# Two-half cross attention in wide steps, three low parts in four on GpSimd and the fourth on VectorE

## The chip, the cores and the metric

The kernel runs on one core of a Trainium2 chip. The metric is the device time of one execution in microseconds (us); a lower figure is better. TensorE (PE) multiplies, VectorE (DVE), ScalarE (ACT) and GpSimd (POOL) work on elements, and SyncE (SP) issues the DMAs.

## The reference

Three residual blocks follow each other on x of 8 batches x 64 queries x 2048 features. The change is in the first one:

```
x = x + xattn(layernorm(x), ctx)      # ctx: 8 x 1601 keys x 2048
    a = einsum('bqd,bkd->bqk', query, key)
    e = softmax(a)
    c = einsum('bqk,bkd->bqd', e, key)   # the keys are the values too
x = x + self_attention(layernorm(x))  # causal, 32 heads, 64 tokens a batch
x = x + lora_experts(layernorm(x))    # rank-8 experts with top-16 gates
```

Everything is float32. Each float32 operand of a large product is split in two: a high part rounded to the format that TensorE multiplies fast (fp32r), and a low part, operand minus high part. The products of the parts are summed in PSUM.

## The kernel before

**Tiling.** The 1601 keys of a batch are three blocks of 512 (4 tiles of 128 keys) and a tail of 65 keys. For the scores the features must lie on the partitions, so each 128 x 128 tile of the context is transposed by TensorE into PSUM (`ps_t`, a ring of 4 banks); ScalarE copies the bank to `ct_hi`, VectorE subtracts that from the bank into `ct_lo`, and two matmuls (`score`, L656 and L657) multiply both with the transposed queries. A slot is one such set: 4 transposes, one copy, one subtraction of 128 x 512, two matmuls of 512 columns. There are 48 slots a batch and 3 for the tail, and 5 more for the queries and the exponentials. `LAG` is 3: the score of a slot stands three slots behind its transposes.

**Natural pieces.** For the second product the keys are used as they lie in memory, in 52 units a batch of one tile x 512 features: ScalarE writes `nat_hi` (L416), GpSimd writes `nat_lo` (L372), and `product` (L680, L681) has two matmuls of 512 columns a unit. For every thirteenth unit, and every second one near the end, VectorE makes both parts (L561, L562). The ring has 8 units.

**Softmax.** It runs online over the three blocks: a maximum per block, a running maximum (L511), exponentials, and `alpha` to rescale. The upper 64 partitions of every product hold the part from the low weights; each block and column group (512 features) is added to `acc` in SBUF (L527, L532). At the end of a batch the upper half is copied down (L436), added (L576), divided by the row sum and added to x (L577).

**Order.** The order on each engine is written out by hand from the table `TRANS` and runs as a loop over batches 1 to 6 with batch 0, batch 7 and an end turn written out around it. The two other blocks of the kernel follow behind a barrier: `self_attention` starts by loading the last 128 rows of x1 and with the layer norm of all rows. Row statistics of the first 384 rows (L590) are computed in the end turn of the cross attention.

Of the kernel before, what the change touches and what calls it, by code (L numbers as in the profile page):

```python
# [34 lines left out]
SHARE, SHARED = 13, (5,)

END_SHARED = 32


def transposes():  # L40

    base = [("c", 0, c) for c in range(DC)] + [("t", k) for k in range(len(TAILS))]
# [4 lines left out]
    base.insert(31, ("e", 0))  # L50
# [2 lines left out]


TRANS = transposes()
NT = len(TRANS)
assert NT % RING == 0
Q1_AT, E2_AT = TRANS.index(("q", 1)), TRANS.index(("e", 2))
SCORE_STEPS = NBLK * DC + len(TAILS)

SPANS = [(0, 0, BLK, 0, DC), (0, BLK, BLK + TAIL, 1, DC + len(TAILS)),
         (1, 0, BLK, 0, 2 * DC + len(TAILS)), (2, 0, BLK, 1, SCORE_STEPS)]


UNITS = [(j, c, k) for j in range(NBLK) for c in range(NCOL) for k in range(KT + (j == 0))]
NU = len(UNITS)
# [5 lines left out]
EIGHTS = NAT * (NU % (NAT - 1))
assert (NU - EIGHTS) % (NAT - 1) == 0


def nat_slot(u):
    return u % NAT if u < EIGHTS else (u - EIGHTS) % (NAT - 1)


def nat_reuse(u):

    return NAT if NAT - 1 <= u < EIGHTS + NAT - 1 else NAT - 1


def unit_slots():

    at = [[] for _ in range(NT)]

    def spread(units, prev, lo, hi):
        for n, u in enumerate(units):
            at[int(lo + n * (hi - lo) / len(units))].append((u, prev))

    spread(range(FIRST_OF[1] + C1_NOW, FIRST_OF[2]), True, 0, 12)
    spread(range(FIRST_OF[2], NU), True, 12, 34)
    spread(range(0, FIRST_OF[1]), False, 34, 54)
    spread(range(FIRST_OF[1], FIRST_OF[1] + C1_NOW), False, 54, NT)
    return at


UNITS_AT = unit_slots()
NATURAL_AT = [[] for _ in range(NT)]
for _s in list(range(LEAD, NT)) + list(range(LEAD)):

    NATURAL_AT[(_s - LEAD) % NT] += [(_u, _prev and _s >= LEAD) for _u, _prev in UNITS_AT[_s]]
LAST_SLOT = {UNITS[u][:2]: s for s, us in enumerate(UNITS_AT) for u, _ in us if LAST_OF[UNITS[u][:2]] == u}

HALF_AT, READ_AT = {22: 0, 25: 1, 42: 2, 3: 3}, {23: 0, 26: 1, 43: 2, 4: 3}
STATS_AT, EXP_AT, SUM_AT = {26: 0, 43: 1, 4: 2}, {28: 0, 45: 1, 6: 2}, 9  # L110

FOLD_AT = {LAST_SLOT[NBLK - 1, c] + 2: c for c in range(NCOL)}
# [1454 lines left out]
```

## Time and profile before

| | |
|---|---|
| median of 3 runs | 1874.06 us (1871.58 to 1874.44) |
| profiled execution, its span | 1873.4 us |
| cross attention, from its first wide copy to its last score | 14.2 to 665.1 us |
| its end, to the first instruction of self attention | 665.1 to 711.8 us |
| self attention and feed forward | 711.8 to 1873.4 us |
| mean granted clock of TensorE | 0.97 |

The span of the profiled execution lies within the three times. Shares of busy time are an average over the three blocks, which have different limits; the stretches above are to be read by themselves. In a timeline the durations of neighbouring matmuls overlap, so what one costs is the distance from its start to the next start.

### The profile page before, as it was taken

The page shows a single profiled execution, that of the slowest core. Times are in us where ns is not written, and L with a number is a line of the kernel's source. Part 1 is how long each engine was busy: PE and PEld are TensorE (multiplying, and loading weights), DVE is VectorE, ACT ScalarE, POOL GpSimd, SP SyncE. Part 2 cuts the span into 40 slices and gives each one's busy share as a digit, 9 for nine tenths or more (in the row PEclk, how much of TensorE's full clock was granted, in tenths as well). Part 3 has the DMA queues.
Part 4 walks back from the last instruction along what each step waited for, and adds up shares of the span by engine and source line. Part 5 has one row for each costly group of instructions (what it writes and reads, how often), then busy time and mean ns, then how long its engine had stood idle before and what let it go on. Part 6 is the DMA issues. An engine that isn't in the chain of part 4 may idle for free. (4 is left out here: it accounts for less than half of the span.)

```text
span 1873.4 us, 25168 instructions
## 1 busy us (share of the span) xinstructions
PE 1731.9 (92%) x8781; PEld 1400.3 (75%) x8781; DVE 901.3 (48%) x1408; ACT 762.8 (41%) x1237; POOL 887.0 (47%) x474
## 2 busy tenths in 40 slices
PE   7898999989899963999999999999999999978999
PEld 6687877878687742788788887888878788756677
DVE  6898999989998997010220301203012030135523
ACT  4687877778777732122122221221222212110321
POOL 0778777787877762234434344333333333312010
PEclk9999999999999975999999999999999999979999
DMA  9356465555546314132232322323222332311113
GB/s 315 101 192 203 143 215 157 179 168 190 184 151 203 102 67 123 47 88 90 91 89 90 90 90 90 90 90 90 86 93 71 106 92 67 102 55 48 45 68 113
DMA packets 174921, 218.87 MB, mean 117 GB/s; under 512 B 3848, under 2 KB 102152, under 8 KB 171784
## 3 DMA queue, kind: packets, MB, share of 16 engines
q1 hardware_dynamic: 174880, 218.32, 36.3%
q8 instruction: 26, 0.43, 0.1%
q14 instruction: 15, 0.12, 0.0%
HBM read 209.92 MB, written 8.39 MB: 117 GB/s over the span
## 5 line engine op out<-in xcount | busy, mean ns | idle before, releaser
L905 POOL TENSOR_TENSOR sa_w_lo<-sa_raw,sa_w_hi 128x2048 fp32r<-128x2048 f32 x80 | 367.9, 4599 | 624.7 <-ACT sa_w_hi L919 624.7
L372 POOL TENSOR_TENSOR xa_nat_lo<-xa_raw,xa_nat_hi 128x512 fp32r<-128x512 f32 x231 | 309.8, 1362 | 96.6 <-ACT xa_nat_hi L416 95.3
L1045 DVE TENSOR_TENSOR rows<-rows,sa_ps_mm 128x512 f32<-128x512 f32 x128 | 88.1, 688 | 494.0 <-PE sa_ps_mm L759 494.0
L757 PE MATMUL sa_ps_mm<-h_hi,sa_w_hi 128*128 128x512 f32 x768 | 303.9, 396 | 1.4 <-DVE h_lo L980 1.4
L758 PE MATMUL sa_ps_mm<-h_lo,sa_w_hi 128*128 128x512 f32 x768 | 300.0, 391 | 0.0
L759 PE MATMUL sa_ps_mm<-h_hi,sa_w_lo 128*128 128x512 f32 x768 | 300.0, 391 | 0.0
L493 DVE TENSOR_TENSOR xa_ct_lo<-xa_ps_t,xa_ct_hi 128x512 fp32r<-128x512 f32 (+2 forms) x408 | 269.8, 673 | 54.4 <-ACT xa_ct_hi L395 43.7
L395 ACT ACTIVATE xa_ct_hi<-xa_ps_t 128x512 fp32r<-128x512 f32 (+2 forms) x408 | 238.5, 588 | 108.1 <-PE xa_ps_t L628 101.2
L919 ACT ACTIVATE sa_w_hi<-sa_raw 128x2048 fp32r<-128x2048 f32 x80 | 153.0, 1913 | 287.1 <-PE sa_ps_mm L759 287.1
L656 PE MATMUL xa_ps_s<-xa_ct_hi,xa_q_t 128*128 128x512 f32 x384 | 185.5, 483 | 40.6 <-DVE xa_ct_lo L493 35.6
L757 PE MATMUL sa_ps_mm<-sa_w_hi,sa_o_hi 128*128 128x512 f32 x512 | 204.3, 399 | 6.9 <-ACT sa_q_t L951 4.8
L758 PE MATMUL sa_ps_mm<-sa_w_lo,sa_o_hi 128*128 128x512 f32 x512 | 203.3, 397 | 0.0
L759 PE MATMUL sa_ps_mm<-sa_w_hi,sa_o_lo 128*128 128x512 f32 x512 | 203.2, 397 | 0.0
L372 POOL TENSOR_TENSOR xa_nat_lo<-rows,xa_nat_hi 128x512 fp32r<-128x512 f32 x112 | 157.0, 1420 | 87.7 <-ACT xa_nat_hi L416 87.6
L680 PE MATMUL xa_ps_o<-xa_nat_hi,xa_e_t 128*128 128x512 f32 (+1 forms) x416 | 173.8, 418 | 14.6 <-DVE xa_nat_lo L562 7.4
L757 PEld LDWEIGHTS sa_ps_mm<-h_hi,sa_w_hi 128*128 128x128 f32 x768 | 144.9, 189 | 35.4 <-ACT sa_v_t L951 2.3
L759 PEld LDWEIGHTS sa_ps_mm<-h_hi,sa_w_lo 128*128 128x128 f32 x768 | 144.8, 189 | 30.7
L758 PEld LDWEIGHTS sa_ps_mm<-h_lo,sa_w_hi 128*128 128x128 f32 x768 | 145.0, 189 | 29.1
L681 PE MATMUL xa_ps_o<-xa_nat_lo,xa_e_t 128*128 128x512 f32 (+1 forms) x416 | 166.5, 400 | 0.0
L628 PE MATMUL xa_ps_t<-xa_ident,xa_raw 128*128 128x128 f32 x1024 | 154.3, 273 | 0.0
L628 PEld LDWEIGHTS xa_ps_t<-xa_ident,xa_raw 128*128 128x128 f32 x1024 | 126.7, 140 | 33.9 <-issue 0.2
L657 PE MATMUL xa_ps_s<-xa_ct_lo,xa_q_t 128*128 128x512 f32 x384 | 151.8, 395 | 0.0
(184 smaller groups left out, 2450.0 us busy)
## 6 DMA issues: line engine op xcount, KB each, us to landing
xa_raw<-in_ctx SPq DMA_DIRECT2D x64, 1024.0 KB, 5.0
rows<-in_ctx SPq DMA_DIRECT2D x32, 1024.0 KB, 5.6
sa_raw<-in_L_attn_w_q SPq DMA_DIRECT2D x32, 1024.0 KB, 5.8
sa_raw<-in_L_attn_w_o SPq DMA_DIRECT2D x32, 1024.0 KB, 4.9
sa_raw<-in_L_attn_w_k SPq DMA_DIRECT2D x8, 1024.0 KB, 5.1
sa_raw<-in_L_attn_w_v SPq DMA_DIRECT2D x8, 1024.0 KB, 5.0
xa_raw_tail<-in_ctx SPq DMA_DIRECT2D x8, 520.0 KB
xa_xq<-in_x SPq DMA_DIRECT2D x8, 512.0 KB, 4.8
```

Source lines behind the costliest of these rows:

```text
L372: pool.tensor_tensor(nat_lo[0:rows, nat_slot(u), :], src, nat_hi[0:rows, nat_slot(u), :].bitcast(F32), ALU.subtract).then_inc(nat_pool, 1)
L395: act.activation(ct_hi[:, bank, 0:w], ps_t[:, bank, 0:w], ACT.Copy).then_inc(hi_done, 1)
L493: dve.tensor_tensor(ct_lo[:, bank, 0:w], ps_t[:, bank, 0:w], ct_hi[:, bank, 0:w].bitcast(F32), ALU.subtract).then_inc(lo_done, 1)
L628: ins.append(pe.transpose(ps_t[:, bank, k * P:(k + 1) * P], piece(j, g // KT)[:, k, g % KT * P:(g % KT + 1) * P], ident[:]))
L656: pe.matmul(o, q_t[:, g, :], ct_hi[:, bank, :], start=g == 0, stop=False)
L680: pe.matmul(o, e_t[0:rows, j, k, :], nat_hi[0:rows, nat_slot(u), :], start=k == 0, stop=False)
L681: pe.matmul(o, e_t[0:rows, j, k, :], nat_lo[0:rows, nat_slot(u), :], start=False, stop=u == LAST_OF[j, c]).then_inc(pv_done, 1)
L757: pe.matmul(out, hi, mov_hi, start=first, stop=False)
L758: pe.matmul(out, hi, mov_lo, start=False, stop=False)
L759: return pe.matmul(out, lo, mov_hi, start=False, stop=last)
L905: pool.tensor_tensor(w_lo[:, n, :], raw[:, n, :], w_hi[:, n, :].bitcast(F32), ALU.subtract).then_inc(w_lo_done, 1)
L919: act.activation(w_hi[:, n % 2, :], raw[:, n % 2, :], ACT.Copy).then_inc(w_hi_done, 1)
```

## The change

The cross attention is written anew; the other two blocks are the same, except for line numbers. `rsqrt_steps` of the cross attention has 3 iterations for 4.

- The keys of a batch are two halves: 833 keys (4 tiles of 128, 3 of 107) and 768 (6 of 128). A step transposes one feature tile of a whole half: 7 or 6 transposes into a slot of two banks, one copy and one subtraction of 833 or 768 columns, and 4 score matmuls (512 and 322, or 512 and 256 columns, for the high and the low part). There are 32 steps a batch for 51 slots. The ring `ps_t` has 2 slots for 4, and `LAG` is 2.
- Transposes of queries and exponentials ride in the spare columns of a step's slot (`SIDE`), with no slot of their own.
- Natural pieces are made as pairs of tiles, 128 x 1024 (or 107 x 1024), 26 a batch, in a ring of 4 pairs. ScalarE makes every high part. The low part is GpSimd's, but VectorE's for each pair with number u % 4 == 2 and for the last 8.
- The softmax has two parts a batch for three. The first half's product goes to `acc` by ScalarE. VectorE rescales it into the PSUM bank of the second half's product (`rescale`), ScalarE copies the upper half out (`low`), and VectorE adds it (`fold`) and divides and adds x (`finish`), all with one operand in PSUM. The running maximum is a `tensor_scalar`.
- The result is stored by column group. The code is written out for all 8 batches, with no loop.
- The 12 row statistics of x1 stand behind everything else of the cross attention on VectorE.

The core of the diff:

```diff
-NBLK = 3
-KT = 4
-RING = 4
-LAG = 3
-SHARE, SHARED = 13, (5,)
-NAT = 8
+HALVES = 2
+TILES = [[128] * 4 + [107] * 3, [128] * 6]
+RING = 2
+LAG = 2
+NAT = 4
+ENDING = before_half(STAGES - 1, PAIRS_OF) + NAT
+ON_DVE = [u >= ENDING or u % 4 == 2 for u in range(len(PAIR_ORDER))]
...
-        ps_t = ps("xa_ps_t", [P, RING, 512])
-        ps_s = ps("xa_ps_s", [P, 2, 512])
+        ps_t = ps("xa_ps_t", [P, RING, 1024])
+        ps_s = ps("xa_ps_s", [P, 1024])
         ps_o = ps("xa_ps_o", [P, 2, 512])
...
+            for u, (h, n) in enumerate(PAIR_ORDER):
+                if ON_DVE[u]:
+                    continue
+                src, p = pair(h, n)
+                pool.wait_ge(nat_act, u + 1)
+                pool.tensor_tensor(nat_lo[0:p, u % NAT, :, :], src, nat_hi[0:p, u % NAT, :, :].bitcast(F32),
+                                   ALU.subtract).then_inc(nat_pool, 1)
...
+            def rescale(b, c):
+                dve.wait_ge(pv_done, uses_before(HALVES * b + 1) + GROUP_END[1][c] + 1)
+                dve.wait_ge(first_out, NCOL * b + c + 1)
+                dve.scalar_tensor_tensor(out=group_bank(c), in0=acc[:, column(c)], scalar=alpha[:, 0:1], in1=group_bank(c),
+                                         op0=ALU.mult, op1=ALU.add).then_inc(rescaled, 1)
+            def fold(b, c):
+                dve.wait_ge(low_ready, NCOL * b + c + 1)
+                dve.tensor_tensor(ps_o[0:LQ, c % 2, :], ps_o[0:LQ, c % 2, :], low[:, c % 2, :], ALU.add).then_inc(folded, 1)
+            def natural_low(u, h, n):
+                src, p = pair(h, n)
+                dve.wait_ge(nat_act, u + 1)
+                dve.tensor_tensor(nat_lo[0:p, u % NAT, :, :], src, nat_hi[0:p, u % NAT, :, :].bitcast(F32),
+                                  ALU.subtract).then_inc(nat_dve, 1)
...
+                if t == ALL_STEPS - 1:
+                    dve.wait_ge(rows_in, 16 * (RT - 1))
+                    for r in range(RT - 1):
+                        for c in range(NCOL):
+                            dve.bn_stats(row_bn[:, r, c, :], x1_rows[:, r, column(c)])
...
+            for t in range(ALL_STEPS):
+                if t == LAG:
+                    first_queries()
+                if t % DC == 2:
+                    for h, i in USE_AT.get(t, []):
+                        product(h, i)
+                if LAG <= t < STEPS + LAG:
+                    score_step(t - LAG)
+                if t < STEPS:
+                    i = transpose_step(t)
+                if t in SIDE:
+                    i = side_step(t)
+                if t < STEPS or t in SIDE:
+                    i.then_inc(t_done, 1)
+                if t % DC != 2:
+                    for h, i in USE_AT.get(t, []):
+                        product(h, i)
```

On TensorE, in the middle of a batch, the rows before are slots of four transposes, two scores (L656, L657) and one unit (L680, L681), here at the end of batch 0's turn:

```order
L628 MATMUL xa_ps_t<-xa_ident,rows 128x128 x4
L648 REGISTER_ALU
L656 MATMUL xa_ps_s<-xa_ct_hi,xa_q_t 128x512
L657 MATMUL xa_ps_s<-xa_ct_lo,xa_q_t 128x512
L673 REGISTER_ALU
L678 REGISTER_ALU
L680 MATMUL xa_ps_o<-xa_nat_hi,xa_e_t 128x512
L681 MATMUL xa_ps_o<-xa_nat_lo,xa_e_t 128x512
```

The rows now, in the second half of a batch: a step's four scores (L611), the six transposes of a later step (L574), four more transposes of queries that ride along (L583), and a pair of units (L631).

```order
L611 MATMUL xa_ps_s<-xa_ct_hi,xa_q_t 128x512
L611 MATMUL xa_ps_s<-xa_ct_hi,xa_q_t 128x256
L611 MATMUL xa_ps_s<-xa_ct_lo,xa_q_t 128x512
L611 MATMUL xa_ps_s<-xa_ct_lo,xa_q_t 128x256
L574 MATMUL xa_ps_t<-xa_ident,xa_raw_b 128x128 x6
L583 MATMUL xa_ps_t<-xa_ident,xa_xq 128x64 x4
L631 MATMUL xa_ps_o<-xa_nat_hi,xa_e_t 128x512
L631 MATMUL xa_ps_o<-xa_nat_lo,xa_e_t 128x512
L631 MATMUL xa_ps_o<-xa_nat_hi,xa_e_t 128x512
L631 MATMUL xa_ps_o<-xa_nat_lo,xa_e_t 128x512
```

The same columns go through in fewer and larger groups; only one group of transposes stands between a step's transposes and its score, for two before.

On VectorE, within a batch before (L493 is the subtraction for the scores, L561 and L562 the two parts of a unit, L576 and L577 the finish of a column group):

```order
L532 SCALAR_TENSOR_TENSOR xa_acc<-xa_acc,xa_alpha,xa_ps_o 128x512
L493 TENSOR_TENSOR xa_ct_lo<-xa_ps_t,xa_ct_hi 128x512
L561 CAST xa_nat_hi<-rows 128x512
L562 TENSOR_TENSOR xa_nat_lo<-rows,xa_nat_hi 128x512
L493 TENSOR_TENSOR xa_ct_lo<-xa_ps_t,xa_ct_hi 128x512
L576 TENSOR_TENSOR xa_res<-xa_acc,xa_res 64x512
L577 SCALAR_TENSOR_TENSOR xa_res<-xa_res,xa_total,xa_xr 64x512
L493 TENSOR_TENSOR xa_ct_lo<-xa_ps_t,xa_ct_hi 128x512 x4
```

And now (L524 is that subtraction, L494 `rescale`, L499 `fold`, L505 `finish`, L511 the low part of a pair, L455 the normalization of the next queries):

```order
L511 TENSOR_TENSOR xa_nat_lo<-xa_raw_a,xa_nat_hi 107x1024
L455 TENSOR_SCALAR xa_xq<-xa_xq,xa_mv,xa_rs_w 64x512
L524 TENSOR_TENSOR xa_ct_lo<-xa_ps_t,xa_ct_hi 128x768
L527 TENSOR_TENSOR xa_e_t<-xa_ps_t,xa_e_t 107x3x64
L494 SCALAR_TENSOR_TENSOR xa_ps_o<-xa_acc,xa_alpha,xa_ps_o 128x512
L455 TENSOR_SCALAR xa_xq<-xa_xq,xa_mv,xa_rs_w 64x512
L524 TENSOR_TENSOR xa_ct_lo<-xa_ps_t,xa_ct_hi 128x768
L499 TENSOR_TENSOR xa_ps_o<-xa_ps_o,xa_low 64x512
L524 TENSOR_TENSOR xa_ct_lo<-xa_ps_t,xa_ct_hi 128x768
L505 SCALAR_TENSOR_TENSOR xa_acc<-xa_ps_o,xa_total,xa_xr 64x512
L524 TENSOR_TENSOR xa_ct_lo<-xa_ps_t,xa_ct_hi 128x768
```

The finish has its operand in PSUM in place of two in SBUF, and the one operation with both operands in SBUF that is left, besides the normalization with its one, is L511.

On VectorE at the end of the cross attention before, the row statistics (L590) stand between the last units and finishes; L712 is the first instruction of self attention:

```order
L590 BN_STATS row_bn<-rows 128x6 x2
L532 SCALAR_TENSOR_TENSOR xa_acc<-xa_acc,xa_alpha,xa_ps_o 128x512
L576 TENSOR_TENSOR xa_res<-xa_acc,xa_res 64x512
L577 SCALAR_TENSOR_TENSOR xa_res<-xa_res,xa_total,xa_xr 64x512
L590 BN_STATS row_bn<-rows 128x6 x2
L532 SCALAR_TENSOR_TENSOR xa_acc<-xa_acc,xa_alpha,xa_ps_o 128x512
L576 TENSOR_TENSOR xa_res<-xa_acc,xa_res 64x512
L577 SCALAR_TENSOR_TENSOR xa_res<-xa_res,xa_total,xa_xr 64x512
```

And now, with L558 for the statistics and L659 for the first instruction of self attention:

```order
L505 SCALAR_TENSOR_TENSOR xa_acc<-xa_ps_o,xa_total,xa_xr 64x512
L494 SCALAR_TENSOR_TENSOR xa_ps_o<-xa_acc,xa_alpha,xa_ps_o 128x512
L499 TENSOR_TENSOR xa_ps_o<-xa_ps_o,xa_low 64x512
L505 SCALAR_TENSOR_TENSOR xa_acc<-xa_ps_o,xa_total,xa_xr 64x512
L558 BN_STATS row_bn<-rows 128x6 x12
L204 UNCONDITIONAL_BRANCH
L914 UNCONDITIONAL_BRANCH
L659 BN_AGGR sa_mv<-row_bn 128x2 x3
```

All twelve now stand behind the last finish.

## Rows read from the trace of the kernel before

**Rows 1.** The page: busy time of each engine over the span

```profile
PE 1731.9 (92%) x8781; PEld 1400.3 (75%) x8781; DVE 901.3 (48%) x1408; ACT 762.8 (41%) x1237; POOL 887.0 (47%) x474
```

**Rows 2.** Windows: length, then busy us by engine; the first is one batch long

```profile
185.90:268.55 82.65, 77.59 (x471) 62.94 (x470) 76.13 (x123) 63.30 (x123) 65.03 (x49) 1.00 0.55 176
...
14.20:665.10 650.90, 610.27 (x3686) 496.36 (x3686) 586.16 (x920) 492.11 (x955) 488.15 (x363) 1.00 0.54 176
665.10:711.80 46.70, 21.24 (x60) 12.00 (x59) 40.65 (x57) 10.68 (x20) 18.71 (x13) 0.69 0.14 48
```

**Rows 3.** Waits from 103.6 to 678.1 us: total, times, longest

```profile
PEld xa_ps_s L656 <- DVE xa_ct_lo L493: 40.4, 33, 1.8
...
PEld xa_ps_t L639 <- issue: 7.9, 21, 0.7
```

**Rows 4.** Timeline of TensorE: one slot with a unit, then tail pieces

```profile
301.48 0.60 PE L628 MATMUL xa_ps_t<-xa_ident,xa_raw 128*128 128x128 f32 x4
301.84 0.48 PE L656 MATMUL xa_ps_s<-xa_ct_hi,xa_q_t 128*128 128x512 f32 x1
302.15 0.39 PE L657 MATMUL xa_ps_s<-xa_ct_lo,xa_q_t 128*128 128x512 f32 x1
302.38 0.40 PE L680 MATMUL xa_ps_o<-xa_nat_hi,xa_e_t 128*128 128x512 f32 x1
302.62 0.39 PE L681 MATMUL xa_ps_o<-xa_nat_lo,xa_e_t 128*128 128x512 f32 x1
302.85 0.60 PE L628 MATMUL xa_ps_t<-xa_ident,xa_raw 128*128 128x128 f32 x4
...
31.57 0.54 PE L634 MATMUL xa_ps_t<-xa_ident,xa_raw_tail 66*128 66x66 f32 x6
31.91 0.48 PE L656 MATMUL xa_ps_s<-xa_ct_hi,xa_q_t 128*128 128x512 f32 x1
...
34.47 0.28 PE L662 MATMUL xa_ps_s<-xa_ct_hi,xa_q_t 128*128 128x66 f32 x1
34.58 0.28 PE L663 MATMUL xa_ps_s<-xa_ct_lo,xa_q_t 128*128 128x66 f32 x1
```

**Rows 5.** Groups by form: count, busy us, mean ns

```profile
L493 DVE TENSOR_TENSOR xa_ct_lo<-xa_ps_t,xa_ct_hi 128x512 fp32r<-128x512 f32 x384 | 258.6, 684 | 53.9 <-ACT xa_ct_hi L395 43.2
L395 ACT ACTIVATE xa_ct_hi<-xa_ps_t 128x512 fp32r<-128x512 f32 x384 | 227.4, 595 | 105.9 <-PE xa_ps_t L628 101.2
L489 DVE TENSOR_TENSOR xa_e_t<-xa_ps_t,xa_e_t 128x256 fp32r<-128x256 f32 x24 | 10.0, 417 | 1.6
L395 ACT ACTIVATE xa_ct_hi<-xa_ps_t 128x330 fp32r<-128x330 f32 x16 | 7.0, 440 | 1.5 <-PE xa_ps_t L634 0.7
```

**Rows 6.** Single lines: duration in ns, least, median and most

```profile
L577 DVE SCALAR_TENSOR_TENSOR xa_res<-xa_res,xa_total,xa_xr x32: 744/1658/1671, 117.2 to 706.4; 64x512 f32<-64x512 f32 x32
L511 DVE TENSOR_TENSOR xa_run_max<-xa_run_max,xa_mx x16: 151/1791/2434, 68.1 to 672.3; 64x1 f32<-64x1 f32 x16
L532 DVE SCALAR_TENSOR_TENSOR xa_acc<-xa_acc,xa_alpha,xa_ps_o x64: 721/737/746, 91.3 to 704.3; 128x512 f32<-128x512 f32 x64
L372 POOL TENSOR_TENSOR xa_nat_lo<-xa_raw,xa_nat_hi x231: 1264/1293/1768, 75.9 to 694.3; 128x512 fp32r<-128x512 f32 x116
L905 POOL TENSOR_TENSOR sa_w_lo<-sa_raw,sa_w_hi x80: 4503/4602/4624, 724.2 to 1701.4; 128x2048 fp32r<-128x2048 f32 x80
```

**Rows 7.** Windows of L561, then of L562, over seven batches

```profile
103.60:678.10 574.50, 30.96 (x32) 0.99 0.52 170
...
103.60:678.10 574.50, 31.23 (x32) 0.99 0.52 170
```

**Rows 8.** Timeline of VectorE at the end, and the next block's start

```profile
689.59 1.28 DVE L590 BATCH_NORM_STATS2 row_bn<-rows 128x6 f32<-128x512 f32 x2
...
706.45 0.74 DVE L577 SCALAR_TENSOR_TENSOR xa_res<-xa_res,xa_total,xa_xr 64x512 f32<-64x512 f32 x1
711.85 0.51 DVE L712 BATCH_NORM_AGGREGATE sa_mv<-row_bn 128x2 f32<-128x24 f32 x3 [4.66 <-PEq L160]
```

More of the change, by code:

```diff
@@ L55 @@
[L55 to L68, printed above, removed]
@@ L69 @@
-C1_NOW = 2
-NAT = 8
[L74 to L98, printed above, removed]
-    return at
@@ L102 @@
[L102 to L112, printed above, removed]
@@ new lines, with pair_units, products @@
+NAT = 4
+def pair_units():
+    first = []
+    for c in range(0, NCOL, 2):
+        first += [(c, 0), (c, 2), (c, 4), (c, 6), (c + 1, 0), (c + 1, 2), (c + 1, 4)]
+    second = [(c, k) for c in range(NCOL) for k in (0, 2, 4)]
+    return [first, second]
+def products():
+    out = []
+    for x in range(HALVES):
+        units = {v: n for n, v in enumerate(PAIRS[x])}
+        uses = []
+        for c in range(NCOL):
+            both = [(c, units[c, k], [(k, 0), (k + 1, 1)]) for k in (0, 2, 4)]
+            if x == 0:
+                odd = [(c, units[c - c % 2, 6], [(6, c % 2)])]
+                both = both + odd if c % 2 == 0 else odd + both
+            uses += both
+        out.append(uses)
+    return out
@@ new lines, with before_half @@
+PAIRS = pair_units()
+USES = products()
+PAIRS_OF, USES_OF = [len(p) for p in PAIRS], [len(u) for u in USES]
+LAST_USE = [[max(i for i, v in enumerate(USES[x]) if v[1] == n) for n in range(PAIRS_OF[x])] for x in range(HALVES)]
+GROUP_END = [[max(i for i, v in enumerate(USES[x]) if v[0] == c) for c in range(NCOL)] for x in range(HALVES)]
+def before_half(h, per_half):
+    return sum(per_half) * (h // HALVES) + per_half[0] * (h % HALVES)
+PV_AT = 6
+E_PARTS = [[(4, 0, 4), (5, 4, 7)], [(4, 0, 2), (5, 2, 4), (6, 4, 6)]]
@@ new lines, with evacuations, side_count, product_steps @@
+SIDE = side_transposes()
+def evacuations(t):
+    return min(t, STEPS) + 1
+def side_count(what, n, k):
+    return next(evacuations(t) for t, v in SIDE.items() if v[0] == what and v[1] == n and v[2] <= k < v[3])
+def product_steps():
+    at, step_of = {}, {}
+    for h in range(STAGES):
+        n = USES_OF[h % HALVES]
+        for i in range(n):
+            t = DC * (h + 1) + PV_AT + (i * DC // n if h < STAGES - 1 else i)
+            at.setdefault(t, []).append((h, i))
+            step_of[h, i] = t
+    return at, step_of
@@ L292, in links_per_turn, with column, uses_before, pair @@
-        def links_per_turn():
-            own = sum(shared(0, u) for u in range(NU))
-            return own + (1 + 2 + 2) + 3 + NCOL + (1 + 1 + RSQRT_LINKS)
+        def column(c):
+            return slice(c * 512, (c + 1) * 512)
+        def uses_before(h):
+            return before_half(h, USES_OF)
+        def pair(h, n):
+            x = h % HALVES
+            c, k = PAIRS[x][n]
+            if k == 6:
+                return raw[x][0:TILES[x][k], c:c + 2, k, :], TILES[x][k]
+            return raw[x][0:TILES[x][k], c, k:k + 2, :], TILES[x][k]
@@ L354, in _ @@
-            turns(sp, turn)
-            sp.wait_ge(stored, 16 * B)
+                for h, c in groups_before(t, 4):
+                    b, x = divmod(h, HALVES)
+                    if x == 1:
+                        sp.wait_ge(finished, NCOL * b + c + 1)
+                        sp.dma_start(x1[b * LQ:(b + 1) * LQ, column(c)], acc[0:LQ, column(c)]).then_inc(stored[c], 16)
+                        if c == NCOL - 1 and b + 1 < B:
+                            load_rows(b + 1, xr, xr_in)
+            for c in range(NCOL):
+                sp.wait_ge(stored[c], 16 * B)
@@ L594, in _ @@
[L594 to L604 removed]
+            for i in layernorm_links():
+                link(i)
+            for c in range(NCOL):
+                normalize(c)
```

745 lines of the change are left out of this document (323 added, 422 removed).

## The prediction

> **What bounds the kernel now.** I read the page first [rows 1]: TensorE is busy 92% of the span, but that is a mean over three blocks, and the change is in one of them. So I cut the span into windows [rows 2]. The cross attention takes 650.9 us for its copies and scores and 46.6 us for its end; the 1161.6 us behind it are two blocks whose code the change leaves alone. One batch takes 82.65 us here; I use 82.4, a little under it, as 650.9 us over eight are 81.4 and the first batch starts without products, and there VectorE is busy 76 us (92%), TensorE 77.6, GpSimd 65 and ScalarE 63. TensorE's busy time counts overlaps, so I count its work by starts in the timeline [rows 4]: four transposes and what follows to L656 take 0.36 us, L656 0.31, L657 and each matmul of a unit 0.23. A slot without a unit is 0.90 us. Six tail transposes take 0.34 us, and a 66-column matmul 0.11.
>
> A batch on TensorE is then 48 x 0.90 = 43.4 us for slots, 16 x 0.057 = 0.9 us for tail transposes, 32 x 0.11 = 3.5 us for tail scores, 104 x 0.23 = 23.9 us for units, and 29 small transposes, priced like the wide ones at 0.09 us, 2.6 us: 74.3 us. Against 82.4 us that leaves 8.1 us in which TensorE waits or is held up. The waits [rows 3] say for whom: L656 waits 40.4 us over seven batches (5.8 us each) for the subtraction `xa_ct_lo` on VectorE, and 7.9 us (1.1 each) are issue gaps at the exponentials. So two things set the pace: TensorE's own columns, and hold-ups on VectorE that outlast the ring.
>
> What holds VectorE up is in the single lines [rows 6]. L577 can take 744 ns and has a median of 1658; L511 works on one column, can take 151 ns and has a median of 1791. Both have all operands in SBUF. L532, with one operand in PSUM, is 721 to 746 ns in all 64 cases. The extra time looks like a wait for the end of a GpSimd instruction, which takes 1293 ns.
>
> **The change, part by part.**
>
> *TensorE.* A 833-column step has 7 transposes, scores of 512, 322, 512 and 322 columns; 322 columns at 0.23 us for 512 are 0.145 us, 256 are 0.115. Transposes cost between 0.0875 us (0.35/4) and the 0.11 us of the narrow matmul [rows 4]. The step is 7 x 0.0875 + 0.31 + 0.145 + 0.23 + 0.145 = 1.44 us at the low end and 1.52 at the high end; the 768-column step 1.295 to 1.35. Sixteen of each are 43.8 to 45.9 us, for 47.8 before. Units and small transposes stay at 26.5. A batch is 70.3 to 72.4 us; I take 71.3, a saving of 3.0 us.
>
> *VectorE, without hold-ups.* By the slope between 256 and 512 columns [rows 5], 1.04 ns a column, the subtractions are 1.02 and 0.95 us; back to back about 0.08 us of each vanishes (two L590 of 0.68 take 1.28 us [rows 8]). 32 of them are 29 us for 33: 4 less. From the 76 us go further 8.9 us for L561 and L562 (62.2 over seven batches [rows 7]), 3.6 for the hold-ups of four L577 (1658 - 744 ns), 3.3 for those of two L511, and 5.2 for eight of the twelve 128 x 512 operations on `acc` (0.65 each; L532 shows the size), of which ScalarE takes four and the third block four: 76 - 4 - 8.9 - 3.6 - 3.3 - 5.2 = 51 us, in which the remaining hold-ups of the normalization still are. One block less in the softmax is offset by wider instructions. The new low parts are 6.5 a batch of 1024 columns, 0.68 + 512 x 1.04 ns - 0.08 = 1.14 us: 7.4. The sum is 58 to 59 us.
>
> *VectorE's hold-ups.* Left are 6.5 low parts and 4 normalizations a batch that have all operands in SBUF. A GpSimd instruction of 1024 columns, between the 1293 ns for 512 and the 4602 for 2048 [rows 6], is 1.29 + 512 x 2.15 ns = 2.4 us. The bounds of a hold-up are nothing, if GpSimd has just finished, and 2.4 us. A pair comes every 2.8 to 3 us (26 a batch), longer than 2.4, so GpSimd often is through when VectorE's turn (u % 4 == 2) comes. I take 0.6 us each, 6 us a batch; VectorE then has 65 us, under TensorE's.
>
> *ScalarE.* By the slope between 330 and 512 columns [rows 5], 0.85 ns, a step's copy is 0.87 or 0.81 us, and a pair's high part 1.05. With about 0.1 us less when back to back: 24 + 25 us, softmax and side pieces 6, new copies of `acc` and `low` 4, 59 us for 63. It stays under the rest, but a step on it with a pair and a copy to `low` (0.8 + 1.0 + 0.5 = 2.3 us) is as long as a step.
>
> *The ring.* This is what the change gives away. Between a step's transposes and its score TensorE now has the products of a step (0.75), a score (0.8), transposes (0.7) and products (0.75): 3.0 us. The two evacuations need 0.1 + 0.87 + 1.02 = 2.0, so 1.0 us is spare. Before it was three slots of 1.37, 4.1 us, against 1.4: 2.7 spare. Hold-ups of a microsecond, hidden before, now reach TensorE. I charge per batch: 1.0 us for each of two softmax steps, in which ScalarE waits for VectorE's maximum with the next copy behind it; 0.5 us for each of the 6.5 steps with a low part on VectorE; 1 us for pairs late from GpSimd; 1.1 us of issue gaps as before. That is 7.4 us, for 8.1 now. Its bounds are 1 us (the issue gaps alone) and more than today's, below.
>
> A batch is 71.3 + 7.4 = 78.7 us, against 82.4: 3.7 x 8 = 30 us saved.
>
> *The end.* Before, 42.1 us pass from the last score (665.1) to the end of the last finish (707.2), and 4.6 us from there to self attention (711.85) [rows 2, 8]. Now: softmax 4.5 us (copy 0.8, add 0.9, maximum 1.4, exponentials 1.0, hops), exponentials transposed and split 2 us, then 12 uses. Four pairs are ready; the other eight need ScalarE (1.05) and VectorE, whose eight low parts and twelve other operations are 9 + 8 us, with waits for the banks in between some 22 us. The last finish ends about 29 us behind the last score, 13 us earlier. Behind it come the 12 statistics, 12 x 0.6 = 7.2 us, which lay in gaps before; the store runs beside them, and the barrier (taken as half of the 4.6 us) follows. That gives back 5 us. Net: 8 us saved, with bounds 0 and 12.
>
> *Nothing.* The first wide copy waits for the first layer norm as before; the context's data are the same bytes, and 176 GB/s over the stretch [rows 2] leave the DMA under six tenths busy. The pieces come back 7 steps (16 us) before they are needed. If that cover were gone, a late piece would cost its transfer, 1.6 MB at 176 GB/s or 9 us.
>
> **Sum.** 30 + 8 = 38 us off the profiled 1873.4, and the profiled execution is 0.7 us under the median: 1836 us. A time within 0.2% (3.7 us) of before can't be told from no change.
>
> **Rivals.**
>
> *A. VectorE becomes the bound (slower).* The low parts and normalizations meet GpSimd in mid-instruction each time. 10.5 hold-ups of up to 2.4 us are 25 us; with 59 of work and 2 us of waits for ScalarE a batch takes 86 us, 3.6 more than now: +29, less 8 at the end, 1895 us. It decides from a mean hold-up of about (82.4 - 59 - 2) / 10.5 = 2.0 us. For it speaks that L511's median is longer than a whole GpSimd instruction [rows 6]; against it, that GpSimd has 19.5 pairs x 2.4 = 47 us of work in 79, where before it was 65 in 82 [rows 2]. The Trainium skill (SBUF — State Buffer, "SBUF: two separate sides") says that VectorE and GpSimd share a port pair as an exclusive lock for a whole instruction, the loser blocked; the trace agrees with it in L511 and L577, and taken at its worst, with each meeting a full one, it is this rival. The same page excepts what runs on VectorE's own ports; L532 at 721 to 746 ns agrees.
>
> *B. The shallow ring eats the saving.* Waits rise from 8.1 to about 10.5 us a batch, since every hold-up over 1 us shows. A batch is 81.8 us: 5 + 8 saved, 1861 us. For it: the spare falls from 2.7 to 1.0 us. Against: half of the hold-ups go away.
>
> *C. The waits nearly vanish.* With VectorE at 65 and ScalarE at 59 us nothing but TensorE's columns is left, 71.3 + 3.5: 61 + 8 saved, 1804 us. For it: the waits before were for VectorE alone [rows 3]. Against: steps of ScalarE and VectorE as long as TensorE's own.
>
> **How the numbers follow.** My forecast (78.7 us a batch, its own range 1815 to 1852) has 0.50, B 0.20, C 0.13, A 0.17. The predicted time is the forecast's. For 8 in 10 the range takes B whole and the upper half of C, and of A the mild third: 1802 to 1885. Of B a quarter falls within 0.2%: same 0.05. Slower is A, 0.17, with 0.01 for B's edge: 0.18. Faster 0.77.
>
> **What would show it.** Right: a batch of 77 to 80 us in the windows; L532's kind at 0.74 us, fold and finish without hold-ups; 1024-column GpSimd instructions of 2.4 us; twelve statistics in some 7 us behind the last finish. Wrong: the low parts on VectorE with a median over 2.5 us (A), waits for `xa_ct_lo` above 8 us a batch (B), or waits under 3 us (C). Pairs waited for from GpSimd by more than 2 us a batch would say that a lead of four pairs is too little, which I charged at 1 us only.

## The result, and the profile after

The changed kernel takes 2526.08 us (median of 4 runs, 2525.89 to 2527.45), the kernel before 1874.21 (4 runs, 1871.58 to 1874.44): 1.349 times as long, 95% interval 1.347 to 1.351. The forecast was 1836, the range 1802 to 1885, and no rival ended above 1895. The transfers, which the prediction put down at nothing, set the time of the first block.

The page of the changed kernel, the same rows as in [rows 1] and those that changed most (parts 1, 2, 5 and 6):

```profile
PE 1797.7 (71%) x8781; PEld 1477.0 (59%) x8781; DVE 778.9 (31%) x1130; ACT 752.6 (30%) x928; POOL 736.5 (29%) x250
...
PEclk8587686876967769678696899999999999998999
DMA  2321232322423224232233222232322232231012
GB/s 78 96 77 56 96 109 64 122 75 73 132 64 118 79 73 130 63 104 81 66 133 101 67 84 85 83 98 83 100 83 86 87 93 83 83 100 67 36 67 100
...
L574 PE MATMUL xa_ps_t<-xa_ident,xa_raw_a 128*128 128x128 f32 (+1 forms) x896 | 144.9, 314 | 560.5 <-DMA xa_raw_a<-in_ctx 560.5
...
xa_raw_a<-in_ctx SPq DMA_DIRECT2D x32, 642.0 KB
...
xa_xq<-in_x SPq DMA_DIRECT2D x8, 512.0 KB, 38.7
```

Over the first 1320 us, which are the cross attention but for its end, TensorE is busy 51% and each of the other engines under 40%. TensorE stood 560.5 us in front of the transposes of the first half, waiting for a DMA. Yet the DMA engines are busy two or three tenths. Many loads cannot be the cause; a load that few of them carry can. The 642 KB load is the one of the three tiles of 107 keys.

Two windows, the first one batch long, as in [rows 2] (busy us of PE, PEld, DVE, ACT and POOL, granted clock, DMA share, GB/s); the second view, apart, is the DMA from 200 to 260 us in 40 slices:

```profile
570.73:730.61 159.88, 85.71 (x471) 71.67 (x471) 61.44 (x88) 61.62 (x84) 47.44 (x21) 0.77 0.29 92
...
350.00:360.00 10.00, 7.72 (x48) 6.40 (x46) 4.87 (x6) 6.41 (x9) 7.23 (x4) 1.00 0.07 26
```

```profile
GB/s 25 26 26 26 134 385 194 25 26 26 26 25 26 26 26 25 26 26 26 25 26 26 26 55 310 339 33 26 26 25 37 26 26 25 26 26 26 25 26 26
```

A batch takes 159.9 us, where it took 82.65. Between short peaks above 300 GB/s the transfer rate is flat at 26 GB/s, with 0.07 of sixteen engines busy. One in sixteen is 0.06, so one engine is carrying everything. 642 KB at 26 GB/s are 25 us, four times a batch, 32 in all. On trn2 the Trainium skill ("DMA: Bandwidth & Descriptors", "Why a DMA increments its semaphore by 16 and not by 1") gives a rule of which I took no account: a hardware-issued copy goes over the largest number of engines, 16 at most, that divides the outermost dimension of both its patterns. By that rule a load over 107 partitions, a prime number, has one engine; the trace agrees.

The waits of the changed kernel from 100 to 1200 us, as in [rows 3] (total, times, longest), and the queue of SyncE (start, length of the issue):

```profile
PE xa_ps_t L574 <- DMA xa_raw_a<-in_ctx: 440.4, 25, 19.8
DVE xa_bn L445 <- DMA xa_xq<-in_x: 174.8, 7, 71.0
...
PEld xa_ps_s L611 <- DVE xa_ct_lo L524: 60.5, 14, 49.9
```

```profile
183.26 54.13 SPq L323 DMA_DIRECT2D xa_raw_a<-in_ctx  x6
237.44 25.08 SPq L326 DMA_DIRECT2D xa_xq<-in_x  x1
```

The second damage is in the queue. Six issues took 54 us and the one of the query rows behind them 25 more, although these rows are small and land 5.1 us after their issue in the median where no such load is ahead of them (the kernel with 112 rows below). Here they land 38.7 us after it, VectorE waits for them (174.8 us), and behind that wait in VectorE's order stand the low parts that TensorE needs. The granted clock is 0.77 in this batch, and TensorE's busy time 85.7 us for the 77.6 before. Two rows of its timeline show why, the first behind a wait of 16.9 us, the second four microseconds on. The granted clock is 0.50 (1.2 GHz) from 215 to 219 us and 0.98 (2.4 GHz) from 219.5 to 221.5; from their start to the next matmul the same seven transposes take 1.31 us at the lower level and 0.65 at the higher:

```profile
215.26 1.62 PE L574 MATMUL xa_ps_t<-xa_ident,xa_raw_a 128*128 128x128 f32 x7 [16.85 <-DMA xa_raw_a<-in_ctx]
...
219.66 0.88 PE L574 MATMUL xa_ps_t<-xa_ident,xa_raw_a 128*128 128x128 f32 x7
```

At the end the statistics and the barrier are to be seen. VectorE's timeline, as in [rows 8] (start, length, count, idle before and releaser):

```profile
1356.40 0.74 DVE L505 SCALAR_TENSOR_TENSOR xa_acc<-xa_ps_o,xa_total,xa_xr 64x512 f32<-64x512 f32 x1
1357.07 7.20 DVE L558 BATCH_NORM_STATS2 row_bn<-rows 128x6 f32<-128x512 f32 x12
1364.58 0.69 DVE L659 BATCH_NORM_AGGREGATE sa_mv<-row_bn 128x2 f32<-128x24 f32 x3 [0.30 <-PEq L204]
```

### The profile page after: what moved, and what is told of

Read it like the earlier page. It is cut to its first block and busy times, and to the rows that moved or that the text cites. A ratio compares the mean times of both kernels' runs of the same rounds, so it can differ in the third digit from the quotient of the medians.

```text
span 2524.2 us, 21640 instructions
## 1 busy us (share of the span) xinstructions
PE 1797.7 (71%) x8781; PEld 1477.0 (59%) x8781; DVE 778.9 (31%) x1130; ACT 752.6 (30%) x928; POOL 736.5 (29%) x250
## 5 line engine op out<-in xcount | busy, mean ns | idle before, releaser
L574 PE MATMUL xa_ps_t<-xa_ident,xa_raw_a 128*128 128x128 f32 (+1 forms) x896 | 144.9, 314 | 560.5 <-DMA xa_raw_a<-in_ctx 560.5
L574 PEld LDWEIGHTS xa_ps_t<-xa_ident,xa_raw_a 128*128 128x128 f32 (+1 forms) x896 | 130.8, 172 | 577.2 <-issue 569.9
L413 ACT ACTIVATE xa_ct_hi<-xa_ps_t 128x833 fp32r<-128x833 f32 (+1 forms) x256 | 214.7, 839 | 781.0 <-PE xa_ps_t L574 590.3
L524 DVE TENSOR_TENSOR xa_ct_lo<-xa_ps_t,xa_ct_hi 128x833 fp32r<-128x833 f32 (+1 forms) x256 | 252.9, 988 | 613.9 <-ACT xa_ct_hi L413 407.1
L374 POOL TENSOR_TENSOR xa_nat_lo<-xa_raw_a,xa_nat_hi 128x1024 fp32r<-128x1024 f32 (+1 forms) x84 | 199.9, 2388 | 440.7 <-ACT xa_nat_hi L388 440.7
L374 POOL TENSOR_TENSOR xa_nat_lo<-xa_raw_b,xa_nat_hi 128x1024 fp32r<-128x1024 f32 x66 | 158.3, 2403 | 535.6 <-ACT xa_nat_hi L388 535.4
L611 PE MATMUL xa_ps_s<-xa_ct_hi,xa_q_t 128*128 128x512 f32 (+2 forms) x512 | 156.7, 390 | 81.8 <-DVE xa_ct_lo L524 59.5
L631 PE MATMUL xa_ps_o<-xa_nat_hi,xa_e_t 128*128 128x512 f32 (+1 forms) x416 | 201.8, 485 | 8.9 <-DVE xa_acc L505 6.3
L631 PE MATMUL xa_ps_o<-xa_nat_lo,xa_e_t 128*128 128x512 f32 (+1 forms) x416 | 181.0, 435 | 0.0
L611 PEld LDWEIGHTS xa_ps_s<-xa_ct_hi,xa_q_t 128*128 128x128 f32 x512 | 99.9, 209 | 116.7 <-DVE xa_ct_lo L524 62.3
## 6 DMA issues: line engine op xcount, KB each, us to landing
xa_xq<-in_x SPq DMA_DIRECT2D x8, 512.0 KB, 38.7
```

Source lines behind the costliest of these rows:

```text
L374: pool.tensor_tensor(nat_lo[0:p, u % NAT, :, :], src, nat_hi[0:p, u % NAT, :, :].bitcast(F32), ALU.subtract).then_inc(nat_pool, 1)
L413: i = act.activation(ct_hi[:, t % RING, 0:w], ps_t[:, t % RING, 0:w], ACT.Copy)
L524: i = dve.tensor_tensor(ct_lo[:, t % RING, 0:w], ps_t[:, t % RING, 0:w], ct_hi[:, t % RING, 0:w].bitcast(F32), ALU.subtract)
L574: i = pe.transpose(ps_t[:, t % RING, OFFS[x][k]:OFFS[x][k] + p], raw[x][0:p, c, k, g % 4 * P:(g % 4 + 1) * P], ident[0:p, 0:p])
L611: i = pe.matmul(ps_s[:, lo:hi], q_t[:, g, :], ct[:, t % RING, lo:hi], start=g == 0 and ct is ct_hi, stop=g == DC - 1 and ct is ct_lo)
L631: ins = pe.matmul(group_bank(c), e_t[0:p, x, k, :], nat[0:p, u % NAT, half, :], start=first and (k, half) == tiles[0] and nat is nat_hi, s ...
```

## Experiments

**One engine, two, fifteen, sixteen.** Theory: the number of rows decides the number of engines. Rivals: three tiles in one load, the shape of the pieces, or sheer DMA traffic. In the first kernel each 107-row load is two, of 96 and 11 rows, and TensorE waits for the count of both (as in the two other splits, its line is left out here):

```diff
-    sp.dma_start(raw[x][0:p, c, k0:k1, :], keys_of(b, x, c, k0, k1, p)).then_inc(raw_in[x][c], 16)
+    for lo, hi in (((0, 96), (96, 107)) if p == 107 else ((0, p),)):
+        sp.dma_start(raw[x][lo:hi, c, k0:k1, :], keys_of(b, x, c, k0, k1, p)[lo:hi]).then_inc(raw_in[x][c], 16)
```

> The load of the 107-row tiles in two DMAs, 96 and 11 rows; nothing else. Theory (a DMA over 107 partitions runs on one DMA engine, 26 GB/s, and 32 of them in a row set the time): the waits of the transposes for the DMA go, and the time falls from 2526 to what the blind working gave, 1802 to 1885 us. Rival 1 (the wide steps with a ring of two are slow by themselves and the loads are only asked for late): still above 2300 us. Rival 2 (two DMAs a piece choke SyncE's queue): three are worse, above 2526 us.

Measured: 1873.68 us (10 runs), ratio to before 1.0005 (0.9995 to 1.0015). The whole loss of 652 us is gone, and besides the load and that count nothing was touched.

In the second the load stays one, with 112 rows; the five extra rows are read and not used:

```diff
+    if p == 107:
+        first = src.ap[0]
+        src = bass.AP(src.tensor, src.offset, [[first[0], 112]] + [list(d) for d in src.ap[1:]])
+        p = 112
```

> The same tiles in one DMA over 112 partitions, 5 rows more than are used. Theory: 112 = 7 x 16 spreads over all engines, so like the split in 96 and 11 within 10 us, with one DMA fewer a piece. Rival 1: above 2300 us. Rival 2 (number of DMAs): exactly as slow as the changed kernel, 2526 us, since the number is the same.

Measured: 1870.02 us (10 runs), ratio 0.9981 (0.9972 to 0.9991). More bytes, 656 us less. I call this one the cured kernel.

The third splits in 106 rows and 1:

> The same tiles in DMAs of 106 rows and 1 row. If the number of engines is the largest one up to 16 that divides the number of partitions, 106 = 2 x 53 gives two engines: some 12 us for each of these loads, 49 us a batch, with 25 us more on those engines for their part of the rest: 74 us a batch, about the length of a batch, and a time between 1840 and 2000 us. If any split of the 107 rows cures it, the time is that of 96 and 11. If only a multiple of 16 is fast and all others run on one engine, about 2520 us.

Measured: 2139.05 us (one run). Its DMA from 200 to 300 us:

```profile
GB/s 200 300 214 52 52 30 283 329 0 62 238 362 20 57 113 405 117 0 151 193 337 66 52 243 207 51 51 51 52 63 319 125 52 51 58 51 192 185 255 72
```

The flat parts are at 51 to 52 GB/s, two engines, for 106 = 2 x 53. One row fewer in the load doubles its rate. The rule was right, the time expected from it too low: 2139 us lies above the 1840 to 2000, and a batch takes 109 us (765.1 from the first to the eighth row total), not 74. The queue is held up here too (nine issues from 246 us take 43.5 us); what share of the 35 us that makes was not separated.

The fourth splits in 105 rows and 2:

> The changed kernel with each piece of 107 rows loaded as 105 + 2 rows. Theory (the number of rows decides over how many DMA engines a load is spread: the largest number up to 16 that divides the rows; measured so far 107 rows at 26 GB/s, 106 rows at 52): 105 = 15 x 7 goes over 15 engines, so the load is as good as whole, and the time is within 5 us of the two cured kernels (96 + 11 rows 1873.7 us, 112 rows 1870.0 us). Rival (an odd or unaligned number of rows is slow as such, or a load needs a multiple of 16 rows): 105 rows behave like 107 or 106, 2139 to 2526 us.

Measured: 1872.4 us (one run). As expected, 105 rows, odd and no multiple of 16, are as good as 112 (1866.9 to 1873.8 us): it is the divisor that counts, not alignment. That fifteen engines carried the load was not read from the trace; the time excludes one and two.

The fifth puts the cost into the kernel before, whose computation stays as it is. Its loads of the second block are cut into 107 and 21 rows (TensorE's count again left out):

```diff
-    sp.dma_start(piece(j, c), ctx_v[b, j, c]).then_inc(raw_in[j * NCOL + c], 16)
+    for lo, hi in (((0, 107), (107, P)) if j == 1 else ((0, P),)):
+        sp.dma_start(piece(j, c)[lo:hi], ctx_v[b, j, c][lo:hi]).then_inc(raw_in[j * NCOL + c], 16)
```

> The kernel before, with the four loads a batch of its second block (128 rows, 1 MB) in 107 and 21 rows. Theory: 856 KB on one engine at 26 GB/s are 33 us, four a batch are 132 us for a batch of 82: above 2250 us, with the loss in waits for the DMA. Rival 1 (the new structure is the cause): within 1% of 1874 us, as the bytes are the same.

Measured: 2759.71 us (one run), 887 us above the 1873.17 us of the kernel before, measured beside it. TensorE's largest wait, from 100 to 1200 us:

```profile
PE xa_ps_t L629 <- DMA xa_raw<-in_ctx: 556.0, 22, 32.1
```

So neither the wide steps nor the shallow ring is needed for the loss: the form of the load makes it. These loads have four tiles each, 856 KB or 33 us at 26 GB/s, and the longest wait is 32.1 us.

**Where the 38 us went.** The cured kernel is the change as I had priced it, and gains 3 us, not 38. VectorE's row totals mark its batches (start, length):

```profile
116.75 0.15 DVE L494 RECIPROCAL xa_total<-xa_total 64x1 f32<-64x1 f32 x1
...
195.72 0.16 DVE L494 RECIPROCAL xa_total<-xa_total 64x1 f32<-64x1 f32 x1
...
278.03 0.15 DVE L494 RECIPROCAL xa_total<-xa_total 64x1 f32<-64x1 f32 x1
...
674.47 0.15 DVE L494 RECIPROCAL xa_total<-xa_total 64x1 f32<-64x1 f32 x1
```

In the kernel before the first of them starts at 104.15 us and the eighth at 678.67. So the start is 12.6 us later, seven batches are 16.8 us shorter (557.7 for 574.5), and from the last total to self attention (711.85 before, 710.84 now) it is 3.2 us longer: 1.0 us less up to self attention. From the first total to the seventh (602.25) a batch is 80.9 us on average, and batches of 79.0 and of 82.3 or more alternate.

*The start.* The order of the loads at the start (SyncE's queue of the cured kernel, then VectorE):

```profile
16.41 16.09 SPq L328 DMA_DIRECT2D xa_raw_b<-in_ctx  x4
32.54 4.26 SPq L331 DMA_DIRECT2D xa_xq<-in_x  x1
```

```profile
49.53 0.69 DVE L450 BATCH_NORM_STATS2 xa_bn<-xa_xq 64x6 f32<-64x512 f32 x1 [14.91 <-DMA xa_xq<-in_x]
50.14 1.00 DVE L529 TENSOR_TENSOR xa_ct_lo<-xa_ps_t,xa_ct_hi 128x833 fp32r<-128x833 f32 x1
```

The query rows of batch 1 are asked for at 32.5 us, behind four loads of 1.5 MB; the kernel before asked at 17.22. VectorE waits 14.9 us for them, with a low part of the ring behind. The edit moves their load ahead of the last three of those pieces:

```diff
-            load_rows(0, xr, xr_in)
-            for c in range(NCOL):
-                load_piece(0, 1, c)
+            load_piece(0, 1, 0)
+            sp.wait_ge(first_q_done, 1)
+            load_rows(1, xq, xq_in)
+            for c in range(1, NCOL):
+                load_piece(0, 1, c)
+            load_rows(0, xr, xr_in)
...
-                if t == 5:
-                    sp.wait_ge(first_q_done, 1)
-                    load_rows(1, xq, xq_in)
```

> The cured kernel (112 rows) with the query rows of batch 1 loaded ahead of the last three second-half pieces of batch 0, instead of behind the residual rows and all four of them. Theory: the 13 us by which the first row total comes later than in the kernel before (116.75 for 103.8 us) are a wait of VectorE for these rows (20.8 us in waits of its statistics, 14.9 at the longest), in which the low parts of the context tiles queue behind it, so TensorE stands 14.8 us at 51 us; with the load ahead of it this wait is gone and the whole kernel is 10 to 15 us faster than the cured one: 1855 to 1860 us. Rival: the start is held by the context pieces themselves (DMA bandwidth at the start), the wait only moves to them: 1866 to 1872 us.

Measured: 1854.63 us (4 runs), ratio 0.9908 (0.9892 to 0.9925), 15.4 us under the cured kernel and 0.4 us under the theory's range; the first row total is at 100.18 us, 16.6 us earlier (a start can differ by two, as is seen with step 20 below). The rival's 1866 to 1872 us are excluded.

*TensorE's own steps.*

> The cured kernel, which makes the high and low parts of the natural pieces only for the first two pairs (left out: all the other copies and subtractions of natural pairs; the products read the first two pairs again). All matmuls, transposes and loads stay. Theory (TensorE's own steps are longer than the forecast's 71.3 us a batch, and waits are few): a batch still takes 77 to 79 us, for 80.9 in the cured kernel. Rival (the natural parts, with the port or the ring between GpSimd, ScalarE and VectorE, are what holds the steps up): a batch falls to 73 us or less, and the whole to about 1815 us.

Measured: 1829.82 us (one run), 76.7 us a batch (460.49 us over six): just under the theory's range, far from the rival. Its timeline shows steps with nothing in the way; the distance from start to start is the cost:

```profile
277.64 0.88 PE L577 MATMUL xa_ps_t<-xa_ident,xa_raw_a 128*128 128x128 f32 x7
278.29 0.63 PE L614 MATMUL xa_ps_s<-xa_ct_hi,xa_q_t 128*128 128x512 f32 x2
278.76 0.54 PE L614 MATMUL xa_ps_s<-xa_ct_lo,xa_q_t 128*128 128x512 f32 x2
279.13 0.88 PE L577 MATMUL xa_ps_t<-xa_ident,xa_raw_a 128*128 128x128 f32 x7
...
281.57 0.88 PE L577 MATMUL xa_ps_t<-xa_ident,xa_raw_a 128*128 128x128 f32 x7
```

A step without products is 1.49 us, one with four product matmuls 2.44, a 768-column step 1.36 (298.26 to 299.62). Sixteen of each and 26 times 0.95 us are 70.3 us. The waits in front of the scores add 0.9 us a batch and the issue gaps 1.7. What is left of 76.7, some 3.8 us, I put down to the 29 small transposes, 0.13 us each. The same timeline bears this out: six transposes with four small ones behind them take 1.13 us (225.19 to 226.32), six alone 0.57 (298.26 to 298.83), so 0.14 for a small one.

*The division of the title.* All low parts but the last eight go to GpSimd:

```diff
-ON_DVE = [u >= ENDING or u % 4 == 2 for u in range(len(PAIR_ORDER))]
+ON_DVE = [u >= ENDING for u in range(len(PAIR_ORDER))]
```

> The cured kernel with the low parts of all natural pairs but the last eight on GpSimd, as if the change had not given every fourth to VectorE. GpSimd's pair takes 2.4 us, 26 pairs in a batch are 62.4 us of 80.9. Theory (the ring of four is fed in time either way, VectorE has room): within 10 us of the cured kernel's 1870 us, to the slower side, since two or three pairs that come close together are then late by up to 2.4 us each: 1870 to 1885 us. Rival (VectorE's share with its hold-ups costs more than it gives): faster than 1865 us.

Measured: 1853.86 us (4 runs), ratio 0.9898 (0.9881 to 0.9914). My theory was wrong in sign: without VectorE's share the kernel is 16.2 us faster, and a batch takes 78.3 us (470.1 over six) for 80.9. GpSimd is busy 373 of those 470 us, and the ring of four is fed in time.

*Which of VectorE's low parts cost.* A batch has 26 pairs, so every fourth falls on other steps in every second batch. The slow batches have one at step 20. There, in the cured kernel, VectorE, then GpSimd, then TensorE:

```profile
236.49 1.20 DVE L516 TENSOR_TENSOR xa_nat_lo<-xa_raw_a,xa_nat_hi 107x1024 fp32r<-107x1024 f32 x1
237.62 2.58 DVE L460 TENSOR_SCALAR xa_xq<-xa_xq,xa_mv,xa_rs_w 64x512 f32<-64x512 f32 x1
240.14 0.94 DVE L529 TENSOR_TENSOR xa_ct_lo<-xa_ps_t,xa_ct_hi 128x768 fp32r<-128x768 f32 x1
```

```profile
237.44 2.49 POOL L379 TENSOR_TENSOR xa_nat_lo<-xa_raw_a,xa_nat_hi 107x1024 fp32r<-107x1024 f32 x1 [2.35 <-ACT xa_nat_hi L393]
```

```profile
241.39 0.62 PE L616 MATMUL xa_ps_s<-xa_ct_hi,xa_q_t 128*128 128x512 f32 x2 [2.21 <-DVE xa_e_t L532]
```

The low part runs free, but it pushes the normalization behind the start of a GpSimd instruction (237.44); that one ends at 239.93 and the normalization at 240.20, though it takes 0.53 us where nothing is in its way. The low part of the ring stands behind both. The edit moves the low parts of this step alone:

```diff
+STEP_20 = {u for t, v in PAIR_AT.items() if t % 32 == 20 for u, _, _ in v}
-ON_DVE = [u >= ENDING or u % 4 == 2 for u in range(len(PAIR_ORDER))]
+ON_DVE = [u >= ENDING or (u % 4 == 2 and u not in STEP_20) for u in range(len(PAIR_ORDER))]
```

> The cured kernel (112 rows) in which only the low parts of step 20 of a batch go from VectorE to GpSimd: four in all, one in every second batch. In the cured kernel the batches with this low part take 82.3 to 83.9 us and the others 79.0: at that step TensorE waits 2.2 us for VectorE, which has the low part (1.20 us) and behind it a normalization held up to 2.58 us while GpSimd is in mid-instruction. Theory (the cost of VectorE's share is this one place, where two long things on VectorE follow each other): all batches take about 79 us, 4 x 3.3 = 11 to 14 us off 1870: 1856 to 1859 us. Rival (every low part on VectorE costs TensorE about 0.4 us, 2.5 us in 6.5, wherever it stands): 4 of some 50 moved, 1.6 us off, 1868 us.

Measured: 1860.92 us (4 runs), ratio 0.9937 (0.9921 to 0.9954): 9.1 us under the cured kernel. The expectation miscounted: the step holds three low parts, not four (the three slow batches), so the theory's figure would have been 3 x 3.3 = 10 us and the rival's 1.2. The slow batches fall to 80.0 us (193.46 to 273.43), not quite to 79.0. At the same place VectorE now shows:

```profile
234.23 1.39 DVE L461 TENSOR_SCALAR xa_xq<-xa_xq,xa_mv,xa_rs_w 64x512 f32<-64x512 f32 x1
```

The normalization takes 1.39 us for 2.58, and TensorE's next scores (from 236.81 us) wait 0.33 us for VectorE, for 2.21. Counted between row totals, the three slow batches are 8.5 us shorter together. The profiled run gains another 2.3 us ahead of its first row total (114.42 for 116.75 us), where the edit changes nothing: VectorE waits 13.0 us for the query rows at the start, for 14.9. So the start can differ by two microseconds without the edit, and part of the 9.1 may be that. The six batches took 485.5 us in the cured kernel and 470.1 with all low parts on GpSimd, 15.4 less. Step 20 makes 8.5 of them, more than half; if the costs add, the other 36 low parts in these batches share the remaining 7, about 0.2 us each.

**A version that beats both.** It has the early query rows, the low parts on GpSimd, and five of the twelve statistics in VectorE's gaps (four behind `finish` of the third column, one behind the last `rescale`).

> The cured kernel (112 rows) with three edits together: query rows of batch 1 loaded early (alone -15.4 us), all low parts but the last eight on GpSimd (alone -16.2 us), and five of the twelve row statistics moved into VectorE's gaps before the last finish (four behind the third column's finish, one behind the last rescale). Theory (the costs lie in different places, so the gains add; statistics of 0.6 us each, five hidden): 1870 - 15.4 - 16.2 - 3.0 = 1835 us, within 3. Rival (earlier start and faster batches meet in the same wait, or the statistics delay the last column's chain): 1840 to 1850 us.

Measured: 1838.96 us (5 runs), ratio 0.9819 (0.9806 to 0.9833). The gains add up to within 4 us of the sum: a little outside the theory's 3 us, and short of the rival's 1840. What the five statistics give by themselves was not measured.

> As the kernel with the three edits, but two of the last eight low parts (the second and the sixth) go to GpSimd too. Theory: VectorE is what the end waits for between the fourth and eighth of these pairs (1.21 us each, back to back with rescales, folds and finishes), GpSimd idles there; two fewer save VectorE 2.4 us, of which 1 to 2 us reach the last finish: 1 to 2 us faster than the other, about 1833 us. Rival: a GpSimd pair takes 2.4 us and comes later than VectorE's would have, and TensorE's products are in order: 0 to 2 us slower.

Measured: 1837.06 us (5 runs), ratio 0.9809 (0.9795 to 0.9822), 1.9 us under the other (1836.27 to 1838.16 for 1838.65 to 1840.33): the difference as in the theory, both kernels 4 us above the expected figures. VectorE's end in it:

```profile
671.89 0.74 DVE L510 SCALAR_TENSOR_TENSOR xa_acc<-xa_ps_o,xa_total,xa_xr 64x512 f32<-64x512 f32 x1
672.56 4.23 DVE L526 BATCH_NORM_STATS2 row_bn<-rows 128x6 f32<-128x512 f32 x7
677.10 0.51 DVE L674 BATCH_NORM_AGGREGATE sa_mv<-row_bn 128x2 f32<-128x24 f32 x3 [0.30 <-PEq L204]
```

## Why the prediction was wrong, step by step

**The failed step is "Nothing."** It said that the context's data are the same bytes, that 176 GB/s leave the DMA under six tenths busy [rows 2], and priced a late piece at 1.6 MB over 176 GB/s, 9 us. The mean rate belongs to loads of 128 rows. A load of 107 rows runs at 26 GB/s: 25 us for its 642 KB alone, longer than the 16 us of cover on which I relied. Same bytes, other form. The kernel with 96 + 11 rows takes 652 us less, of the 690 between forecast and result; those with 112, 105 + 2 and 106 + 1 rows say that the divisor does it. The other 38 us lie in the steps below. That a batch took 160 us, when four such loads make 101, I explain by the issues held up in SyncE's queue and by the lower clock; their shares were not separated.

The other steps are read in the cured kernel.

- **TensorE, 71.3 us a batch.** 74.1 us, the batch of the kernel without natural parts less its waits (76.7 - 0.9 - 1.7). The mechanism was right and the term too small in three places: the 32 wide steps are 45.6 us for the 44.8 in the middle of my bounds (1.49 us for 1.44 to 1.52, 1.36 for 1.295 to 1.35), the products 24.7 for 23.9, and the 29 small transposes, priced at 0.09 us like the wide ones, some 3.8 for 2.6. My upper bounds were also added up wrongly: at 0.11 us a transpose the steps are 1.60 and 1.43 us, not 1.52 and 1.35, and their sum is 48.5 us a batch, not 45.9; the middle of the right bounds, 72.6 us for a batch, would have been nearer. (Smaller slips: 48 x 0.90 is 43.2, not 43.4; the four transposes of [rows 4] take 0.36 us, not 0.35; seven steps of a batch of 78.7 us are 17 us, not 16.)
- **GpSimd's pair, 2.4 us.** Measured 2.39 us.
- **VectorE's hold-ups, 0.6 us for each of 10.5.** From 100 to 640 us low parts are 1.22 us in the median, 1.20 at least and 1.30 at most, so none to speak of; normalizations are 1.31 us on average (0.53 at least), 0.8 each. Together some 3 us for 6. Rival A as a whole is refuted: VectorE is busy 373 of 485 us, 62 us a batch for the 65 of my sum. But its mechanism costs 8.5 us at one step. That a normalization is held by GpSimd is read from where the two end, and from its shorter time when it starts elsewhere; no run took GpSimd away alone.
- **The ring, 7.4 us of waits.** By difference 80.9 - 74.1 = 6.8 us. The natural pieces make 4.2 of them (80.9 - 76.7), for the 4.3 charged, and softmax and issue gaps 2.6 for 3.1. The sizes were about right; that the low parts' share lies mostly at one step was not foreseen.
- **The batch, 78.7 us.** 80.9: the 2.2 us are the columns of the first point, less 0.6. Rival B's 81.8 was nearer in number, but not its mechanism: it had 10.5 us of waits for the 6.8. The 1870 us of the cured kernel lie inside my range, but partly by luck, as the late start is in none of its terms.
- **The end, 8 us saved.** About 1 saved: TensorE's last score matmul starts at 665.25 us, and from there to self attention it is 45.6 us, for 46.7. The last finish ends 38 us behind the last score, where I had 29: the softmax and its transposes took 9 us to the row total, for 6.5, and the products behind it 29 for 22, with waits of TensorE for the banks (3.4 us at 689) and of VectorE for the last products (2.9 us at 701). One low part on VectorE, ahead of the last softmax, takes 2.72 us for 1.22 (665.26 us), and the granted clock is 0.50 from 671 to 676.5 us; neither is in my terms. The statistics took 7.20 us as worked out. The barrier costs 0.30 us, not 2.3; that the 4.6 us of [rows 8] were the wait for the last store, which now lies beside the statistics, was not tried.
- **A step that the prediction does not have.** The load of the next query rows behind 6 MB of second-half context at the start, 15.4 us. I had counted every instruction of a batch, but not the order of SyncE's queue before the first one.

## What to carry to other kernels

Price a load by its outer dimension before its bytes: where a tile's number of rows has no divisor near 16, load it as a multiple of 16 and a rest, or over a few rows too many. Low DMA shares beside long waits for a DMA are the sign, and a flat GB/s row gives the number of engines. An operation that is cheap where it stands may still push the next one into a meeting with another engine: look at the steps where two such things stand behind one another, and at SyncE's queue from its first entry.

## What the hardware showed that was not expected

- One DMA engine carried 25 to 26 GB/s and two carried 51 to 52, at 107 and 106 rows of three pieces of 2 KB each. A load of 112 rows landed in 7.3 us in the median.
- A load on one engine holds up the queue that issues it: single issues of the first half's pieces took up to 26.5 us (2.7 at most with 112 rows), and a load of 512 KB behind them took 25 to 28 us to issue in six of the eight batches.
- The row `[0.30 <-PEq L204]`: a barrier between two blocks cost 0.3 us on VectorE when its own statistics came last.
- Behind self attention's first instruction the same code took 1161.6 us before, 1159.6 in the changed and 1158.1 us in the cured kernel. Of the 4.5 us between the profiled executions of the kernel before and the cured one, 3.5 lie here. TensorE's granted clock goes with them: it is 0.50 until some 38 us behind that instruction in the cured kernel (0.62 from 745 to 750 us, 1.00 from 750 on), and until 44 us behind it in the kernel before (0.50 from 751 to 756 us, 0.84 from 756 to 761). Why it rises earlier was not looked into.
